# Quantising the last layer's weights during the expert layer, and loading them rounded

## Chip, cores and metric

One core of one Trainium2 chip runs the whole program in one launch. The metric is device time in microseconds (us), lower is better. The kernel before has a median of 3632.83 us over three runs (3630.29 to 3636.98).

## What is computed

x has 8 batches of 512 rows of 256 values; a context of 8 x 1024 x 192 is attended to. Four sublayers follow one another, each added to x after a layer norm: a cross attention of 16 heads, an expert layer (for each batch the two best of eight experts, chosen from the batch's first row, two 256 x 256 matrices each with GELU between), a second cross attention, and a quantised feed-forward layer, which is where the change begins:

```python
def quantize_w8_per(w, axis):
    amax = jnp.clip(jnp.max(jnp.abs(w), axis=axis, keepdims=True), 1e-08, None)
    scale = 127.0 / amax
    return jnp.clip(jnp.round(w * scale), -128.0, 127.0) / scale
...
W_in_sim = quantize_w8_per(W_in, axis=0)      # 256 x 1024
W_out_sim = quantize_w8_per(W_out, axis=1)    # 1024 x 256
x_sim = quantize_a16(x)                       # one scale for all of x
hidden = jax.nn.gelu(x_sim @ W_in_sim + b_in, approximate=False)
hidden_sim = quantize_a16(hidden)             # one scale for all of hidden
out = hidden_sim @ W_out_sim + b_out
```

The quantised weights depend on the inputs alone, so they can be made at any time before the layer.

## The kernel before, in words

`build` runs four functions one behind the other, each a block in which the five engines have their own instruction streams, tied by semaphores: `first_attention`, `experts` (L860), `second_attention` (L1112) and `quantised_layer` (L1721). All DMAs around the change are issued by SyncE (SP) on one queue.

**experts.** SyncE loads eight first rows for the routing (L926), x of batch 0 (L927), two small routing arrays (L928, L929) and x of the other seven batches, 512 KB each, which share one semaphore (L931). Then it waits for the routing, stores the chosen numbers as one row of 256 bytes (L935), waits for it and loads, batch by batch into two sets of buffers, the weights of two experts (L945 to L951). VectorE does the routing, normalises batch 0, and then in a loop normalises batch b+1 and updates batch b:

```python
with dve.Fori(0, B - 1) as b:
    normalise_batch(b + 1)
    update(b)
```

A normalisation is statistics (L72, L78, L81), a reciprocal root on GpSimd (L1086) and the scaling (L89). GpSimd then takes half of the second bias off x (L1097 to L1103). TensorE does for each batch: the hidden product (L987), the turning of the next batch's normalised rows (`turn_rows`, L973), the second product (L998). ScalarE applies GELU (L1025) and keeps the turned rows in SBUF (L1014). Batches go in pairs, in a loop of three with the last pair unrolled; TensorE's turned rows for batch b+1 need the normalisation that stands behind the update of batch b-1 on VectorE.

**second_attention.** In the last batch SyncE loads the turned first weight matrix, 1 MB, into the resident buffer `spare` (L1286), and it stores every batch's x as it is done (L1288).

**quantised_layer.** In its first block SyncE waits for the stores of x and loads x again (L1842 for batches 0 and 1, L1845 for the other six, under one semaphore), the two biases (L1847, L1848), and, once `spare` is free, the second matrix into it (L1851). VectorE first quantises the first matrix in `spare` (`quantise_weights`, L1731 to L1753: maximum per row, scale, eight multiplications L1746, clipping and rounding L1751 and L1753), then normalises the eight batches and takes their maxima (L72 to L1900). TensorE turns the rounded matrix in two halves of eight 128 x 128 transposes (L1861), each copied by ScalarE (L1880), and then the rows of x (L1872, L1883). After x's overall maximum (L1792 to L1808) the second block multiplies: VectorE rounds x (L1951, L1954) and splits off the low part (L1959), ScalarE makes the high part (L2008) and the GELU (L2014), TensorE the first projection (L1999). VectorE's order there is: batches 0 and 1 rounded and split, the second matrix quantised in `spare`, and then a loop that rounds batch b+2, takes the maxima of batch b's GELU (L1966) and splits batch b+2. The third block multiplies with the second matrix (L2186, L2188).

Of the kernel before, what the change touches and what calls it, by code (L numbers as in the profile page):

```python
# [5 lines left out]
F32 = mybir.dt.float32  # L6
# [7 lines left out]
P = 128  # L14
# [845 lines left out]
def experts(nc, x_sb, ident, mhalf, d, x_before):  # L860

    with ExitStack() as ctx:
# [33 lines left out]
        hT = sb("hT", [P, 2, FT, NQ])  # L896

# [21 lines left out]
        s_x = sem("x_updated")  # L919

# [3 lines left out]
        def _(sp):  # L924
# [12 lines left out]
            with sp.Fori(0, B // 2) as i:  # L937
                for u in range(2):

                    sp.wait_ge(s_x, QT * (2 * i + u))  # L940
                    for k in range(2):
# [10 lines left out]
                                     ).then_inc(s_w[u], 16)  # L952

        @block.tensor
        def _(pe):
# [11 lines left out]
            def turn_rows(b):  # L967
# [6 lines left out]
                mm.then_inc(s_tr, 1)  # L974

# [30 lines left out]
            with pe.Fori(0, B // 2 - 1) as i:  # L1006
                two_batches(i, False)
# [3 lines left out]
        def _(act):  # L1011
# [19 lines left out]
            with act.Fori(0, B // 2 - 1) as i:  # L1031
# [4 lines left out]
        def _(dve):  # L1036
# [37 lines left out]
            with dve.Fori(0, B - 1) as b:  # L1074
# [37 lines left out]
def second_attention(nc, x_sb, ident, ident_r, mhalf, d, ctx_parts, x_dram, spare, s_win, s_xs):  # L1112


    with ExitStack() as ctx:
# [112 lines left out]
        def _(sp):  # L1228
# [39 lines left out]
            def batch(b, left):  # L1268
# [452 lines left out]
def quantised_layer(nc, ident, ones, mhalf, d, x_dram, out, spare, s_win, s_xs):  # L1721
# [5 lines left out]
    with ExitStack() as ctx:  # L1727
        def sb(name, shape, dt=F32, to=ctx):
            return to.enter_context(nc.sbuf_tensor("f_" + name, shape, dt))

        def quantise_weights(dve, w, whole, top, s, inv, loaded, need, s_wq):  # L1731


            dve.wait_ge(loaded, need)
            nc.vector.tensor_reduce(top[:], w[:], AX.X, ALU.max, apply_absolute_value=True
                                    ).then_inc(s_wq, 1)
            dve.wait_ge(s_wq, 1)
            nc.vector.tensor_scalar(top[:], top[:], TINY, None, ALU.max).then_inc(s_wq, 1)
            dve.wait_ge(s_wq, 2)
            nc.vector.reciprocal(s[:], top[:]).then_inc(s_wq, 1)  # L1740
            dve.wait_ge(s_wq, 3)
            nc.vector.tensor_scalar(s[:], s[:], 127.0, None, ALU.mult).then_inc(s_wq, 1)
            dve.wait_ge(s_wq, 4)
            nc.vector.reciprocal(inv[:], s[:]).then_inc(s_wq, 1)
            for t in range(FFT):
                nc.vector.tensor_scalar(w[:, t, :], w[:, t, :], s[:, t:t + 1], -128.0,  # L1746
# [548 lines left out]
```

## Time and profile before

| | |
|---|---|
| median of 3 runs | 3632.83 us (3630.29 to 3636.98) |
| profiled execution, its own time | 3637.8 us |
| its span in the trace | 3635.9 us |
| TensorE busy, matmul | 3342.1 us (92% of the span) |
| VectorE | 2393.1 us (66%) |
| ScalarE | 1674.5 us (46%) |
| GpSimd | 1207.1 us (33%) |
| DMA | 379.08 MB, mean 104 GB/s |

PE is TensorE's matmuls, PEld its weight loads, DVE VectorE, ACT ScalarE, POOL GpSimd, and SPq the DMA instructions that SyncE issues. The span runs from the first to the last instruction of one profiled execution; the time of that execution is 1.9 us longer. The granted clock is 1.00 where TensorE runs at 2.4 GHz and 0.50 where it runs at 1.2 GHz; a number between is a stretch with both. The experts take the span from about 2109 to 2265 us, the second attention to 3384, the last layer the rest. A busy share is an average; which wait ends last is read from the timelines.

### The profile page before, as it was taken

The page shows a single profiled execution, that of the slowest core. Times are in us where ns is not written, and L with a number is a line of the kernel's source. Part 1 is how long each engine was busy: PE and PEld are TensorE (multiplying, and loading weights), DVE is VectorE, ACT ScalarE, POOL GpSimd, SP SyncE. Part 2 cuts the span into 40 slices and gives each one's busy share as a digit, 9 for nine tenths or more (in the row PEclk, how much of TensorE's full clock was granted, in tenths as well). Part 3 has the DMA queues.
Part 4 walks back from the last instruction along what each step waited for, and adds up shares of the span by engine and source line. Part 5 has one row for each costly group of instructions (what it writes and reads, how often), then busy time and mean ns, then how long its engine had stood idle before and what let it go on. Part 6 is the DMA issues. An engine that isn't in the chain of part 4 may idle for free. (4 is left out here: it accounts for less than half of the span.)

```text
span 3635.9 us, 49119 instructions
## 1 busy us (share of the span) xinstructions
PE 3342.1 (92%) x14300; PEld 1881.8 (52%) x14300; DVE 2393.1 (66%) x3634; ACT 1674.5 (46%) x1904; POOL 1207.1 (33%) x545
## 2 busy tenths in 40 slices
PE   6999999999999999999999868799999999999576
PEld 4445445455454464454464445455555555554366
DVE  4665665665656656656646524687788778777699
ACT  3442442443433433434434312366566566566376
POOL 2563663554645545636546613100000000000101
PEclk9999999999999999999999989799999999999698
DMA  7444544444534435535445232344344343343202
GB/s 183 122 119 117 121 121 103 121 109 126 121 101 123 120 101 133 122 99 125 108 118 128 68 110 79 75 105 106 72 102 104 79 103 96 89 101 82 65 18 75
DMA packets 265102, 379.08 MB, mean 104 GB/s; under 512 B 35944, under 2 KB 170672, under 8 KB 265008
## 3 DMA queue, kind: packets, MB, share of 16 engines
q1 hardware_dynamic: 265008, 378.06, 41.2%
q8 instruction: 31, 0.51, 0.1%
q14 instruction: 63, 0.52, 0.0%
HBM read 82.22 MB, written 27.26 MB: 30 GB/s over the span
## 5 line engine op out<-in xcount | busy, mean ns | idle before, releaser
L839 POOL TENSOR_TENSOR a_prob_sum<-a_prob_sum,a_prob 128x1024 f32<-128x1024 f32 x384 | 915.8, 2385 | 420.4 <-ACT a_prob L576 409.6
L576 ACT ACTIVATE a_prob<-a_t 128x1024 f32<-128x1024 f32 x512 | 518.8, 1025 | 752.9 <-PE a_t L430 739.5
L1590 DVE TENSOR_REDUCE a_mhalves<-a_m 128x1 f32<-128x512 f32 x1024 | 689.9, 688 | 188.2 <-PE a_m L1341 185.2
L718 DVE TENSOR_REDUCE a_mhalves<-a_m 128x1 f32<-128x512 f32 x1024 | 671.0, 688 | 165.0 <-PE a_m L397 161.8
L1502 ACT ACTIVATE a_prob<-a_t 128x1024 f32<-128x1024 f32 x512 | 498.3, 1023 | 145.5 <-PE a_t L1361 140.2
L397 PE MATMUL a_m<-a_kh_n,a_qz 128*128 128x512 f32 x1024 | 445.1, 457 | 64.1 <-DVE a_kl_n L707 29.3
L1341 PE MATMUL a_m<-a_vh,a_qz 128*128 128x512 f32 x1024 | 463.5, 464 | 36.6 <-DVE a_mhalves L1590 19.7
L437 PE MATMUL a_o<-a_prob,a_v_pair 128*64 128x512 f32 x2048 | 495.7, 605 | 0.0
L732 DVE RECIPROCAL a_recip<-a_x 128x512 f32<-128x512 f32 x64 | 214.8, 3357 | 349.0 <-PE a_x L446 349.0
L397 PEld LDWEIGHTS a_m<-a_kh_n,a_qz 128*128 128x128 f32 x1024 | 186.3, 192 | 367.9 <-DVE a_mhalves L718 223.5
L422 PE MATMUL a_t<-a_q_hl,a_k_hh 128*128 128x512 f32 x1024 | 360.3, 433 | 8.0 <-DVE a_x_res L787 8.0
L1341 PEld LDWEIGHTS a_m<-a_vh,a_qz 128*128 128x128 f32 x1024 | 189.9, 189 | 325.1 <-DVE a_mhalves L1590 246.6
L430 PE MATMUL a_t<-a_q_hm,a_k_lm 66*128 66x512 f32 x1024 | 326.8, 400 | 0.0
L1361 PE MATMUL a_t<-a_qs,a_vs 128*128 128x512 f32 x1024 | 323.2, 397 | 3.9 <-ACT a_prob L1502 3.6
L1703 POOL TENSOR_TENSOR a_rstd<-a_veps,mhalf 128x4 f32<-128x4 f32 x8 | 8.1, 1018 | 820.0 <-DVE a_veps L81 819.8
L1368 PE MATMUL a_o<-a_prob,a_v_all 128*18 128x512 f32 x2048 | 269.7, 598 | 0.4 <-ACT a_prob L1502 0.4
L422 PEld LDWEIGHTS a_t<-a_q_hl,a_k_hh 128*128 128x128 f32 x1024 | 191.0, 192 | 117.1 <-issue 74.6
L839 POOL TENSOR_TENSOR a_prob_sum<-a_prob 128x1024 f32<-128x1024 f32 x64 | 153.5, 2398 | 279.0 <-ACT a_prob L576 279.0
L437 PEld LDWEIGHTS a_o<-a_prob,a_v_pair 128*64 128x64 f32 x2048 | 124.2, 136 | 206.2 <-issue 166.0
L1361 PEld LDWEIGHTS a_t<-a_qs,a_vs 128*128 128x128 f32 x1024 | 191.7, 189 | 53.1 <-ACT a_prob L1502 14.4
L430 PEld LDWEIGHTS a_t<-a_q_hm,a_k_lm 66*128 66x128 f32 x1024 | 197.7, 193 | 35.6 <-ACT a_q_hm L594 0.5
L582 ACT CAST a_kh_n<-a_m 128x1024 fp32r<-128x1024 f32 x64 | 64.8, 1012 | 142.7 <-PE a_m L375 142.7
(242 smaller groups left out, 4081.2 us busy)
## 6 DMA issues: line engine op xcount, KB each, us to landing
a_k_hh<-a_kh_n SPq DMA_DIRECT2D x256, 256.0 KB, 4.5
a_k_lm<-a_kl_n SPq DMA_DIRECT2D x128, 256.0 KB, 4.2
a_v_pair<-a_v_all SPq DMA_DIRECT2D x64, 512.0 KB, 3.9
a_vs<-a_vh SPq DMA_DIRECT2D x256, 128.0 KB, 2.3
a_wk<-wk_parts SPq DMA_DIRECT2D x64, 256.0 KB, 3.5
a_q_hl<-a_qz SPq DMA_DIRECT2D x128, 128.0 KB, 3.3
a_q_hm<-a_qz SPq DMA_DIRECT2D x128, 128.0 KB, 3.7
a_q_hl<-a_ql_n SPq DMA_DIRECT2D x128, 128.0 KB, 4.2
```

Of the source, the lines that this page charges most:

```text
L397: pe.matmul(ps_m[:, n, :], qz[:, hd, qt * P:(qt + 1) * P], kh_n[:, n * 512:(n + 1) * 512], start=True, stop=True).then_inc(s_mx, 1)
L422: pe.matmul(ps_t[t % 2][:, hd, :], k_hh[:, u, hd, keys], q_hl[:, u, hd, :], start=True, stop=False)
L430: mm = pe.matmul(ps_t[t % 2][:, hd, :], k_lm[0:HD0 + 2, u, hd, keys], q_hm[0:HD0 + 2, u, hd, :], start=False, stop=True)
L437: mm = pe.matmul(ps_o[hd * HD0:(hd + 1) * HD0, :], v_pair[:, pr.set, t, hd * HD0:(hd + 1) * HD0], prob[:, t % RING, hd, :], start=(t == 0) ...
L576: nc.scalar.activation(prob[:, t % RING], ps_t[t % 2][:, :, :], ACT.Exp, scale=SCALE0).then_inc(s_exp, 1)
L718: nc.vector.tensor_reduce(mhalves[:, qt, hd, n:n + 1], ps_m[:, n, :], AX.X, ALU.max).then_inc(s_max, 1)
L839: nc.gpsimd.tensor_tensor(acc, prob[:, (t - 1) % RING] if t == 1 else acc, prob[:, t % RING], ALU.add).then_inc(s_acc, 1)
L1341: pe.matmul(ps_m[:, k, :], qz[:, u, h, qt * P:(qt + 1) * P], vh[:, u, k * 512:(k + 1) * 512], start=True, stop=True).then_inc(s_mx, 1)
L1361: mm = pe.matmul(ps_t[j][:, h, :], vs[:, u, 2 * j + h, keys], qs[:, u, 2 * j + h, :], start=True, stop=True)
L1368: mm = pe.matmul(ps_o[QD * h:QD * h + VW, :], v_all[:, t, GH * n + h, :], prob[:, t % RB, h, :], start=(t == 0), stop=(t == KT - 1))
L1502: nc.scalar.activation(prob[:, t % RB, 2 * j:2 * j + 2, :], ps_t[j][:, :, :], ACT.Exp, scale=SCALE1).then_inc(s_exp, 1)
L1590: nc.vector.tensor_reduce(mhalfs[:, u, qt, h, k:k + 1], ps_m[:, k, :], AX.X, ALU.max).then_inc(s_max, 1)
```

## The change

In `experts` SyncE now also loads both raw weight matrices (1 MB each), behind x and ahead of the chosen numbers. VectorE's loop is opened for the first two batches: it quantises the first matrix after the update of batch 0 and the second after that of batch 1. TensorE turns the first matrix behind the first pair of batches, in the PSUM tile that otherwise holds turned rows, with ScalarE copying. At the end SyncE stores both rounded matrices in device memory. In `second_attention` the load of the first matrix goes. In `quantised_layer` both quantisations, the turning and the load of the raw second matrix go; SyncE loads the two rounded matrices, 1 MB each, behind x and the biases. The scales' inverses stay in SBUF. `quantise_weights` itself is unchanged but for where it is defined.

```diff
@@ experts, SyncE
             for b in range(1, B):
                 sp.dma_start(x_sb[:, b * QT:(b + 1) * QT, :], x_view[:, b * QT:(b + 1) * QT, :]
                              ).then_inc(s_xrest, 16)
+            sp.dma_start(win_raw[:], d["winT"].rearrange("(t p) k -> p t k", p=P)).then_inc(s_wl[0], 16)
+            sp.dma_start(wout_raw[:], d["wout2"].rearrange("(t p) n -> p t n", p=P)).then_inc(s_wl[1], 16)
 
             sp.wait_ge(s_rt, 8)
             sp.dma_start(chosen_row[:], chosen[:]).then_inc(s_row, 16)
...
+            sp.wait_ge(s_wk, 2)
+            sp.dma_start(win_parts, win[:].bitcast(F32).rearrange("p c k -> p (c k)")).then_inc(s_win, 16)
+            sp.wait_ge(s_wq[1], 15)
+            sp.dma_start(wout_parts, wout[:].bitcast(F32).rearrange("p t n -> p (t n)")).then_inc(s_win, 16)
@@ experts, TensorE
+            def turn_weights():
+                pe.wait_ge(s_wq[0], 15)
+                pe.wait_ge(s_xnT, 3)
+                for r in range(2):
+                    pe.wait_ge(s_wk, r)
+                    for c in range(DCH):
+                        for t in range(4):
+                            mm = pe.transpose(ps_tr[:, c, t * P:(t + 1) * P],
+                                              win_raw[:, 4 * r + t, c * P:(c + 1) * P], ident[:])
+                    mm.then_inc(s_wt, 1)
+                pe.wait_ge(s_wk, 2)
...
-            with pe.Fori(0, B // 2 - 1) as i:
+            two_batches(0, False)
+            turn_weights()
+            with pe.Fori(1, B // 2 - 1) as i:
                 two_batches(i, False)
@@ experts, ScalarE
-            with act.Fori(0, B // 2 - 1) as i:
+            two_batches(0, False)
+            for r in range(2):
+                act.wait_ge(s_wt, r + 1)
+                nc.scalar.copy(win[:, :, r * 512:(r + 1) * 512], ps_tr[:]).then_inc(s_wk, 1)
+            with act.Fori(1, B // 2 - 1) as i:
                 two_batches(i, False)
@@ experts, VectorE
-            with dve.Fori(0, B - 1) as b:
+            normalise_batch(1)
+            update(0)
+            quantise_weights(nc, dve, win_raw, win_raw, win_max, win_s, win_inv, s_wl[0], 16, s_wq[0])
+            normalise_batch(2)
+            update(1)
+            quantise_weights(nc, dve, wout_raw, wout, wout_max, wout_s, wout_inv, s_wl[1], 16, s_wq[1])
+            with dve.Fori(2, B - 1) as b:
                 normalise_batch(b + 1)
                 update(b)
@@ second_attention, SyncE
-                else:
-
-                    sp.wait_ge(s_kq, 3 * NG * B)
-                    sp.dma_start(spare[:], d["winT"].rearrange("(t p) k -> p t k", p=P)).then_inc(s_win, 16)
@@ quantised_layer, first block
-                        sp.wait_ge(s_wt, 2)
-                        sp.dma_start(spare[:], d["wout2"].rearrange("(t p) n -> p t n", p=P)).then_inc(s_wout, 16)
-                        sp.wait_ge(s_wout, 48)
+                        sp.wait_ge(s_win, 32)
+                        sp.dma_start(win[:].bitcast(F32).rearrange("p c k -> p (c k)"), win_parts
+                                     ).then_inc(s_const, 16)
+                        sp.dma_start(wout[:].bitcast(F32).rearrange("p t n -> p (t n)"), wout_parts
+                                     ).then_inc(s_const, 16)
+                        sp.wait_ge(s_const, 64)
...
-                        for r in range(2):
-                            pe.wait_ge(s_wq, 15)
...
-                        quantise_weights(dve, spare, spare, win_max, win_s, win_inv, s_win, 16, s_wq)
@@ quantised_layer, second block
                     low(1, 1)
-                    quantise_weights(dve, spare, wout, wout_max, wout_s, wout_inv, s_mm, 1, s_wq2)
```

## Rows read from the trace of the kernel before

**Rows 1.** windows view, two stages: busy us per engine (x instructions), granted clock, DMA share, GB/s

```profile
2151.00:2183.00 32.00, 29.83 (x113) 19.50 (x112) 15.54 (x36) 8.69 (x11) 9.62 (x8) 1.00 0.27 82
...
3374.00:3400.00 26.00, 12.82 (x64) 8.64 (x56) 16.84 (x47) 4.70 (x6) 2.26 (x2) 0.74 0.55 180
```

**Rows 2.** timeline of one expert batch: start us, us, engine, line, operation, [idle before <- releaser]

```profile
2151.95 7.03 PE L987 MATMUL e_h<-e_xnT,e_w 128*128 x16
...
2152.25 0.43 DVE L1068 SCALAR_TENSOR_TENSOR x_sb<-e_y,x_sb 128x256 f32 x1 [1.30 <-PE e_y L998]
...
2155.96 4.18 DVE L89 TENSOR_SCALAR e_xn<-x_sb,e_mv,e_rstd 128x256 f32 x4 [1.13 <-POOL e_rstd L1086]
...
2160.20 1.09 PE L973 MATMUL e_tr<-ident,e_xn 128*128 128x128 f32 x8 [1.23 <-DVE e_xn L89]
...
2161.13 7.07 PE L998 MATMUL e_y<-e_w,e_hT 128*128 128x256 f32 x32
...
2168.35 0.42 DVE L1068 SCALAR_TENSOR_TENSOR x_sb<-e_y,x_sb 128x256 f32 x1 [1.30 <-PE e_y L998]
```

**Rows 3.** timeline, start of the experts: SyncE's DMA issues, VectorE and the first expert matmul

```profile
2110.44 7.89 SPq L931 DMA_DIRECT2D x_sb<-x_first  x7
...
2118.37 0.78 SPq L935 DMA_DIRECT2D e_chosen_row<-e_chosen  x1
...
2125.81 1.41 DVE L72 BATCH_NORM_STATS2 e_stats<-x_sb 128x6 f32 x4 [7.26 <-DMA x_sb<-x_first]
...
2126.16 0.41 SPq L945 DMA_DIRECT2D e_w<-in_w  x1
...
2133.96 10.20 PE L987 MATMUL e_h<-e_xnT,e_w 128*128 x16 [13.38 <-DMA e_b<-in_b]
```

**Rows 4.** windows view, one microsecond in which x is being loaded

```profile
2120.00:2121.00 1.00, 0.57 (x3) 0.17 (x1) 0.00 (x0) 0.39 (x1) 0.00 (x0) 0.50 1.11 350
```

**Rows 5.** timeline, start of the last layer: VectorE, TensorE, ScalarE and SyncE

```profile
3384.54 2.29 DVE L1735 TENSOR_REDUCE f_win_max<-spare 128x8 f32<-128x2048 f32 x1 [0.87 <-PEq L1115]
...
3392.21 1.40 DVE L72 BATCH_NORM_STATS2 f_stats<-f_hid 128x6 f32<-128x256 f32 x4
...
3392.35 1.97 PE L1861 MATMUL f_w<-ident,spare 128*128 128x128 f32 x8 [9.14 <-DVE spare L1753]
...
3397.49 1.01 ACT L1880 CAST f_win<-f_w 128x1024 fp32r<-128x1024 f32 x1 [2.12 <-PE f_w L1861]
...
3397.48 0.38 SPq L1851 DMA_DIRECT2D spare<-in_wout  x1
...
3401.47 1.41 DVE L72 BATCH_NORM_STATS2 f_stats<-f_hid 128x6 f32 x4 [2.78 <-DMA f_hid<-x_between]
```

**Rows 6.** timeline, the last layer's first projection: VectorE, ScalarE and TensorE

```profile
3445.62 2.28 DVE L1735 TENSOR_REDUCE f_wout_max<-spare 128x8 f32<-128x2048 f32 x1
...
3453.28 0.75 DVE L1951 TENSOR_SCALAR f_xnT<-f_xnT,f_amax_x  x1
...
3454.90 1.16 ACT L2008 ACTIVATE f_x_high<-f_xnT,f_minus_magic 128x1024 fp32r x1 [1.89 <-DVE f_xnT L1954]
...
3461.67 0.50 PE L1999 MATMUL f_h<-f_x_high,f_win 128*128 128x512 f32 x1 [0.96 <-ACT f_hid L2014]
...
3470.34 0.50 PE L1999 MATMUL f_h<-f_x_high,f_win 128*128 128x512 f32 x1 [0.96 <-ACT f_hid L2014]
```

**Rows 7.** windows view: stretches that show the granted clock fall and rise

```profile
2104.00:2109.00 5.00, 0.76 (x4) 0.33 (x2) 0.42 (x1) 0.00 (x0) 0.00 (x0) 1.00 0.31 105
...
2109.00:2110.00 1.00, 0.00 (x0) 0.00 (x0) 0.00 (x0) 0.00 (x0) 0.00 (x0) 0.72 0.03 8
...
2133.00:2140.00 7.00, 6.04 (x7) 2.52 (x8) 0.00 (x0) 1.97 (x2) 3.68 (x3) 0.50 0.66 188
...
2140.00:2144.00 4.00, 4.00 (x11) 1.71 (x10) 0.00 (x0) 1.37 (x2) 0.00 (x0) 0.98 0.01 4
...
3400.00:3403.00 3.00, 0.00 (x0) 0.00 (x0) 1.48 (x6) 0.60 (x1) 0.00 (x0) 1.00 1.11 343
```

More of the change, by code:

```diff
@@ L857, in _, with quantise_weights, experts @@
             batch(B - 1, True)
-def experts(nc, x_sb, ident, mhalf, d, x_before):
+def quantise_weights(nc, dve, w, whole, top, s, inv, loaded, need, s_wq):
+    dve.wait_ge(loaded, need)
+    nc.vector.tensor_reduce(top[:], w[:], AX.X, ALU.max, apply_absolute_value=True
+                            ).then_inc(s_wq, 1)
+    dve.wait_ge(s_wq, 1)
+    nc.vector.tensor_scalar(top[:], top[:], TINY, None, ALU.max).then_inc(s_wq, 1)
+    dve.wait_ge(s_wq, 2)
+    nc.vector.reciprocal(s[:], top[:]).then_inc(s_wq, 1)
+    dve.wait_ge(s_wq, 3)
+    nc.vector.tensor_scalar(s[:], s[:], 127.0, None, ALU.mult).then_inc(s_wq, 1)
+    dve.wait_ge(s_wq, 4)
+    nc.vector.reciprocal(inv[:], s[:]).then_inc(s_wq, 1)
+    for t in range(FFT):
+        nc.vector.tensor_scalar(w[:, t, :], w[:, t, :], s[:, t:t + 1], -128.0,
+                                ALU.mult, ALU.max).then_inc(s_wq, 1)
+    flat = w[:].rearrange("p t k -> p (t k)")
+    whole = whole[:].rearrange("p t k -> p (t k)")
+    dve.wait_ge(s_wq, 13)
+    nc.vector.tensor_scalar(flat, flat, 127.0, MAGIC, ALU.min, ALU.add).then_inc(s_wq, 1)
+    dve.wait_ge(s_wq, 14)
+    nc.vector.tensor_scalar(whole, flat, MAGIC, None, ALU.subtract).then_inc(s_wq, 1)
+def experts(nc, x_sb, ident, mhalf, d, x_before, win_parts, wout_parts, win_inv, wout_inv, s_win):
     with ExitStack() as ctx:
@@ L896, in experts @@
         hT = sb("hT", [P, 2, FT, NQ])
+        win_raw = sb("win_raw", [P, FFT, D])
+        wout_raw = sb("wout_raw", [P, FFT, D])
+        win = sb("win", [P, DCH, FF], F32R)
+        wout = sb("wout", [P, FFT, D], F32R)
+        win_max = sb("win_max", [P, FFT])
+        win_s = sb("win_s", [P, FFT])
+        wout_max = sb("wout_max", [P, FFT])
+        wout_s = sb("wout_s", [P, FFT])
         ps_tr = psum("tr", [P, DCH, NQ])
@@ L1109, in _, with second_attention @@
             two_batches(B // 2 - 1, True)
-def second_attention(nc, x_sb, ident, ident_r, mhalf, d, ctx_parts, x_dram, spare, s_win, s_xs):
+def second_attention(nc, x_sb, ident, ident_r, mhalf, d, ctx_parts, x_dram, spare, s_xs):
     with ExitStack() as ctx:
@@ L1729, in sb @@
             return to.enter_context(nc.sbuf_tensor("f_" + name, shape, dt))
[L1731 to L1746, printed above, removed]
-                                        ALU.mult, ALU.max).then_inc(s_wq, 1)
-            flat = w[:].rearrange("p t k -> p (t k)")
-            whole = whole[:].rearrange("p t k -> p (t k)")
-            dve.wait_ge(s_wq, 13)
-            nc.vector.tensor_scalar(flat, flat, 127.0, MAGIC, ALU.min, ALU.add).then_inc(s_wq, 1)
-            dve.wait_ge(s_wq, 14)
-            nc.vector.tensor_scalar(whole, flat, MAGIC, None, ALU.subtract).then_inc(s_wq, 1)
         def psum(name, shape, to=ctx):
@@ L1877, in _ @@
                     def _(act):
-                        for r in range(2):
-                            act.wait_ge(s_wt, r + 1)
-                            nc.scalar.copy(win[:, :, r * 512:(r + 1) * 512], ps_w[:]).then_inc(s_wk, 1)
                         with act.Fori(0, B) as b:
```

41 lines of the change are left out of this document (16 added, 25 removed).

## Prediction, made before the changed kernel was run

> **What bounds the kernel now.** I read the page first for the size of the whole, then a table of stages, then timelines of the two places that the change touches. The sum below is made against the profiled execution, 3637.8 us (span 3635.9); the median of the three runs shown is 3632.8, 5.0 us less, so what the sum adds is added to the median. 0.2%, about what a measurement of this kernel can tell from no change, is 7.3 us.
>
> The change takes work from the last layer and puts it into the experts. By busy share the experts look like a good home for vector work: in a stretch of two batches VectorE is busy 15.54 of 32 us, while where the last layer starts it is busy 16.84 of 26 us [rows 1]. The shares mislead in both places, and the timelines say why.
>
> In an expert batch one chain closes on itself [rows 2]. The last update of x for batch 0 starts at 2152.25; VectorE then normalises batch 2, its last scaling ending at 2160.14 (2155.96 + 4.18); TensorE turns those rows at 2160.20, after 1.23 us with nothing to do; the second expert product follows at 2161.13; and the next batch's last update starts at 2168.35. The period is 2168.35 - 2152.25 = 16.1 us. The hidden product (7.03 us from 2151.95) lies beside the normalisation and ends before it. So whatever VectorE does between an update and the next normalisation lengthens the chain in full, though VectorE stands idle elsewhere in it, for the second product.
>
> In the last layer the first quantisation runs from 3384.54 to 3392.21, 7.67 us, at the head of VectorE's work [rows 5]. But at 3401.47, before the statistics of batch 2, VectorE has waited 2.78 us for the loads of x. These six loads share one semaphore, so that time is set by the transfers and not by VectorE. The second quantisation runs from 3445.62 to 3453.28, 7.66 us, beside the first projection [rows 6]. There TensorE starts each batch 0.96 us after its own last product of the batch before, when the last GELU is done: 3461.67 and 3470.34 both show that wait, on ScalarE and not on VectorE.
>
> **The change part by part.**
>
> First, SyncE issues two loads of 1 MB (the raw weight matrices) in the experts between the loads of x and the load of the chosen experts' numbers. Now the last x loads are issued by 2118.33, the numbers at 2118.37; they arrive only just before 2126.16, when the first expert weights are issued, though they are 256 bytes [rows 3]. They stand behind the x bytes, which arrive for VectorE at 2125.81; the DMA engines were full then, 350 GB/s [rows 4]. Two more megabytes ahead of them are 2.10 MB / 350 GB/s = 6.0 us. TensorE's first expert product waited for the expert weights until 2133.96 [rows 3], so it starts at about 2140.0: **+6.0 us**. Bounds: 0, if the numbers slip past the bulk; 7.5, if the engines reach only 80% of that rate.
>
> Second, the quantisation of the first matrix stands on VectorE after batch 0's update and before the normalisation of batch 2. It is 15 instructions, the same as now, so 7.67 us [rows 5]. It is on the chain: TensorE turns batch 2's rows that much later, and all behind it (product, update, next normalisation) waits. **+7.7 us.** The second quantisation stands after batch 1's update and before the normalisation of batch 3: 7.66 us [rows 6], **+7.6 us** rounded down, as the hidden product of that batch, which now comes later, may take a little of it over. GpSimd has nothing to do in either stretch: its bias work for batch 1 stands behind the reciprocal root for batch 2, and so meets the scaling as now (4.18 us). Nothing of the 15.3 us is hidden. Lower bound 12, if 3 us somewhere find cover; above, 15.5.
>
> Third, TensorE turns the first matrix, 16 transposes in two halves, each followed by a copy on ScalarE, with TensorE waiting. In the last layer this takes from 3392.35 to 3398.50, 6.2 us [rows 5]. In the experts it follows batch 1's second product, while VectorE updates, quantises (7.7) and normalises (7.5): 15.8 us from that product's end. TensorE needs 6.2 + 7.0 for the next hidden product = 13.2. **0**, with 2.6 us to spare; if VectorE's work were not there, 6.2.
>
> Fourth, the clock. TensorE's hidden product of batch 1 ends at 2158.98 now, 2165.0 then, and the rows it turns next come at 2173.9: 8.9 us of nothing. In this trace 5 us with 0.76 us of work leave it at the full 2.4 GHz, and then it falls, 0.72 in the next microsecond [rows 7]; the same product at 1.2 GHz, before the clock rises at about 2140, takes 10.20 us [rows 3, 7] where it takes 7.03 at full clock [rows 2]. The rows' turning and the second product, which are on the chain, restart at the low level: I take **+3.0 us**, near that difference of 3.2. Bounds: 0 and 4.1 (3.2 and 0.9 for the eight transposes, 1.97 us [rows 5] against 1.09 [rows 2]).
>
> Fifth, two stores of 1 MB are issued at the experts' end, behind the last expert weights, which are issued when batch 5 is updated, so with two batches (2 x 16.1 us) still to run; 6.0 us of transfer: **0**, at most 6 if the next stage's first loads met them.
>
> Sixth, the last layer without the first quantisation, its 16 transposes and two copies. VectorE can take batches 0 and 1 earlier and then waits for the six loads until 3401.47 as before. The 7.67 us become waiting: 2.78 grows to some 9 or 10. **0.** The load of the second matrix, issued at 3397.48, is replaced by two of 1 MB issued some 1.5 us earlier, again behind x, and nothing needs them before the first projection. **0**; bounds 0 and +3, if the two took half of the rate while the last of x is in flight. The removed load in the second attention was hidden: 0.
>
> Seventh, the first projection without the second quantisation. ScalarE's high part for batch 2 waited 1.89 us for VectorE [rows 6] and no longer does, but it had made this up by 3461.67, as TensorE's wait there is the usual 0.96. **-0.1**, with bounds 0 and -1.9.
>
> **Sum:** 6.0 + 7.7 + 7.6 + 0 + 3.0 + 0 + 0 - 0.1 = +24.2 us: 3662.0 for an execution like the profiled one, **3657.0 from the median**.
>
> A rule that bears on the third and fourth term: the three blocks of eight transposes in the last layer were TensorE's only work since 3383, and after them the clock stands at 1.00 from 3400 to 3403 [rows 5, 7], so turning does raise it. The Trainium skill (TensorE: Matmul & The Clock Gate, Part 4: PE-mode transpose) says that the full clock doesn't engage for transposes, which don't count as a busy TensorE. By that rule TensorE would count as idle from batch 1's second product on, and the fourth rival below would be the forecast; the rows contradict it.
>
> **The rivals.**
> A (6%), faster: the experts have the cover. VectorE's idle half there [rows 1] takes both quantisations, the loads slip in, and the last layer gives back both: 3632.8 - 7.7 - 7.7 = 3617.4. Its place is the chain of rows 2: it holds only if TensorE's own work per batch is longer than normalisation plus quantisation, that is if the 1.23 us of waiting were more than 7.7 us of slack instead. And the return needs x to land by about 3394. Half of it would still be faster. The rows speak against both; I leave it 3% for the whole and 3% for a part that ends at no change.
> B (12%): the load of the numbers isn't held up by the matrices: 3657.0 - 6.0 = 3651.0. For it: the DMA engines are sixteen, and a small transfer uses few. Against: the numbers took from 2118.37 to about 2125 now.
> C (8%): x lands sooner or VectorE is the bound of the last layer's start after all. The gain is then what the quantisation took less its old wait, 7.7 - 2.8 = 4.9: 3652.1.
> D (12%): the clock falls a second time, between the matrix's turning (or the hidden product after it) and batch 3's rows, and the chain pays once more: 3657.0 + 3.0 = 3660.0.
>
> **How the numbers follow.** The forecast has 62%, the four rivals 38%. The likeliest case's own range is 3657.0 - 4 (clock at 0, some cover) to + 5 (dearer transfers, stores, clock), and some 0.1% for the spread of the runs. Taking in B, C and D the range is 3648 to 3665; outside are A and chances of a missed term. Slower by over 0.2% is above 3640.1: the forecast, B, C and D, 94%. No change: 3%. Faster: 3%.
>
> **What would show it.** Right: the first expert product at about +6 us against the row of before, the first weights issued at some 2132; gaps of about 8 us on TensorE before the rows of batches 2 and (about 2) 3, each with VectorE in the quantisation; the clock at 0.50 after the first; the experts longer by some 24 us; in the last layer a wait for x of 9 or 10 us before the statistics of batch 2, and the time from the last store of x to the end unchanged within 1 us. Wrong: quantisations that run while TensorE is at the second product, numbers that land at 2125 as now, or a last layer shorter by 5 us or more.

## The result, and the profile after

The changed kernel takes 3674.4 us, the median of 4 runs (3671.7 to 3677.6), against 3631.6 us before (3629.9 to 3637.0): a ratio of 1.0113, 95% interval 1.0098 to 1.0129, **1.1% slower**. The forecast was 3657.0 us, the range 3648 to 3665: right in its sign, and short by 17 us. The profiled execution after has a span of 3669.8 us against 3635.9. It was the fastest of the four after, and the one profiled before was slower than any of the four it is timed against, so the spans differ by 33.9 us where the medians differ by 42.9; the 9 us between the two are in no table below. All executions that the ratios of this document rest on are fast ones; one of run 7's four took 6628 us and is left out of its ratio, though not of its median.

Where the 33.9 us between the two profiled spans went, by the start of VectorE's last addition in each stage (first attention, experts, second attention, last layer), in us. For the first attention it is the first of its four closing additions, 10.3 us ahead of the last in every run, so those 10.3 us count with the experts throughout:

| | first attention ends | experts | second attention | last layer |
|---|---|---|---|---|
| before | 2094.5 | 168.9 | 1119.8 | 249.6 |
| after | 2094.9 | 190.1 | 1134.6 | 247.1 |
| after - before | +0.4 | **+21.2** | **+14.8** | -2.5 |
| forecast | 0 | +24.3 | 0 | -0.1 |

The experts came out 3.1 us under the forecast. The second attention, whose arithmetic the change does not touch, lost 14.8 us, and no term or rival had it: the one sentence of the forecast on that stage is that the load removed there was hidden, 0.

**The start of the experts.** SyncE's queue and TensorE's first rows, timelines of the kernel after (start, us, engine, line, operation, tiles, then idle time before and what ended it):

```profile
2118.32 1.33 SPq L970 DMA_DIRECT2D e_win_raw<-in_winT  x1
2119.69 3.30 SPq L971 DMA_DIRECT2D e_wout_raw<-in_wout  x1
2123.04 2.01 SPq L974 DMA_DIRECT2D e_chosen_row<-e_chosen  x1
2132.43 0.40 SPq L984 DMA_DIRECT2D e_w<-in_w  x1
```
```profile
2139.79 9.76 PE L1042 MATMUL e_h<-e_xnT,e_w 128*128 128x512 f32 x16 [18.85 <-DMA e_b<-in_b]
```

The numbers are issued at 2123.04 where it was 2118.37, the first weights at 2132.43 where it was 2126.16, and the first product starts 5.8 us later [rows 3]. Of 6.3 us of delay, 4.7 lie between the issues of x and that of the numbers, where the two new issues stand (1.33 and 3.30 us), and 1.6 behind it. An issue takes 0.40 us at 2132.43; whether the two are long because the queue is still full of x, and so an effect of the transfers, no run tells.

**The chain of the experts.** VectorE, then TensorE, in the same columns:

```profile
2157.54 0.42 DVE L1129 SCALAR_TENSOR_TENSOR x_sb<-e_y,x_sb 128x256 f32<-128x256 f32 x1 [1.30 <-PE e_y L1053]
2157.88 2.27 DVE L864 TENSOR_REDUCE e_win_max<-e_win_raw 128x8 f32<-128x2048 f32 x1
...
2164.39 1.23 DVE L882 TENSOR_SCALAR e_win_raw<-e_win_raw 128x2048 f32<-128x2048 f32 x1
2165.54 1.40 DVE L72 BATCH_NORM_STATS2 e_stats<-x_sb 128x6 f32<-128x256 f32 x4
...
2168.69 4.17 DVE L89 TENSOR_SCALAR e_xn<-x_sb,e_mv,e_rstd 128x256 f32<-128x256 f32 x4 [1.13 <-POOL e_rstd L1153]
...
2182.38 0.43 DVE L1129 SCALAR_TENSOR_TENSOR x_sb<-e_y,x_sb 128x256 f32<-128x256 f32 x1 [1.30 <-PE e_y L1053]
2182.72 2.28 DVE L864 TENSOR_REDUCE e_wout_max<-e_wout_raw 128x8 f32<-128x2048 f32 x1
...
2190.38 1.40 DVE L72 BATCH_NORM_STATS2 e_stats<-x_sb 128x6 f32 x4
```
```profile
2157.34 7.03 PE L1042 MATMUL e_h<-e_xnT,e_w 128*128 128x512 f32 x16
2172.92 1.97 PE L1016 MATMUL e_tr<-ident,e_xn 128*128 128x128 f32 x8 [8.55 <-DVE e_xn L89]
2174.68 7.66 PE L1053 MATMUL e_y<-e_w,e_hT 128*128 128x256 f32 x32
2182.17 1.04 PE L1026 MATMUL e_tr<-ident,e_win_raw 128*128 128x128 f32 x8
2184.31 1.09 PE L1026 MATMUL e_tr<-ident,e_win_raw 128*128 128x128 f32 x8 [1.10 <-ACT e_win L1091]
```

Each quantisation stands between an update and the next statistics (2157.88 to 2165.54, 2182.72 to 2190.38), 7.66 us each, and TensorE's wait ahead of batch 2's rows grows from 1.23 [rows 2] to 8.55. Now the period from update to update is 24.8 us (2157.54 to 2182.38) in place of 16.1 [rows 2].

TensorE's clock in five stretches of the kernel after. Behind the bounds and the length stand busy us (and instructions) of TensorE's matmuls, its weight loads, VectorE, ScalarE and GpSimd, then the granted clock as a share of 2.4 GHz, DMA share and GB/s:

```profile
2133.00:2145.00 12.00, 5.21 (x6) 2.18 (x7) 0.00 (x0) 1.97 (x2) 3.68 (x3) 0.50 0.70 219
2145.00:2150.00 5.00, 5.00 (x17) 2.52 (x16) 0.00 (x0) 1.79 (x3) 0.00 (x0) 0.99 0.02 6
2169.00:2175.00 6.00, 2.08 (x9) 2.08 (x10) 3.86 (x4) 0.08 (x1) 3.44 (x3) 0.50 0.00 0
2176.00:2186.00 10.00, 8.30 (x46) 7.03 (x44) 4.76 (x10) 1.57 (x2) 0.00 (x0) 1.00 0.14 39
2186.00:2192.00 6.00, 4.91 (x6) 2.19 (x7) 5.88 (x18) 1.14 (x2) 0.00 (x0) 0.51 0.52 157
```

It fell in the 8.55 us of waiting as expected, and again at 2186, behind the turning of the matrix. The first fall cost 1.97 - 1.09 us on the rows and 7.66 - 7.07 on the product. The second cost nothing, since the slow product lay beside VectorE's quantisation and normalisation.

**The last layer.** VectorE's first and third statistics in the kernel after:

```profile
3419.61 0.42 DVE L1725 TENSOR_TENSOR x_sb<-a_m,x_sb 128x256 f32<-128x256 f32 x1 [0.44 <-PE a_m L1523]
...
3427.35 1.41 DVE L72 BATCH_NORM_STATS2 f_stats<-f_hid 128x6 f32<-128x256 f32 x4 [7.31 <-DMA f_hid<-x_between]
...
3438.89 1.41 DVE L72 BATCH_NORM_STATS2 f_stats<-f_hid 128x6 f32 x4 [5.05 <-DMA f_hid<-x_between]
```

The 7.67 us of quantisation have turned into waits for x, 7.31 and 5.05 us where there was one of 2.78 [rows 5], and batch 2's statistics start 19.3 us behind the last addition where it was 18.2 (3401.47 - 3383.25). The 2.5 us that this stage still won are luck. VectorE's first result for the last batch but one starts 240.0 us behind the second attention's last addition in both kernels; over the 7 us of the last products the clock is 0.51 before (3625 to 3632) and 1.00 after (3659 to 3666).

**The second attention.** VectorE at the turn of its loop over the batches (five turns), first before, then after:

```profile
2733.17 0.75 DVE L1662 TENSOR_TENSOR x_sb<-a_m,x_sb 128x256 f32 x2
2735.17 3.27 DVE L1590 TENSOR_REDUCE a_mhalves<-a_m 128x1 f32<-128x512 f32 x5 [1.26 <-PE a_m L1341]
```
```profile
2759.79 0.75 DVE L1725 TENSOR_TENSOR x_sb<-a_m,x_sb 128x256 f32 x2
2763.49 1.29 DVE L1653 TENSOR_REDUCE a_mhalves<-a_m 128x1 f32<-128x512 f32 x2 [2.95 <-issue]
```

A wait of 2.95 us that no semaphore ends ("issue") stands where 1.26 us for TensorE stood. TensorE then waits for VectorE, and its clock halves for some 7 us. TensorE's wait after, then the stretch of 7 us before and after:

```profile
2764.24 0.79 PE L1404 MATMUL a_m<-a_vh,a_qz 128*128 128x512 f32 x1 [1.78 <-DVE a_mhalves L1653]
```
```profile
2735.00:2742.00 7.00, 6.21 (x27) 3.06 (x26) 4.99 (x8) 5.14 (x5) 0.00 (x0) 1.00 0.66 165
```
```profile
2763.00:2770.00 7.00, 5.76 (x19) 3.55 (x19) 4.63 (x7) 4.95 (x5) 0.00 (x0) 0.52 0.65 172
```

A looped batch takes 136.4 us in place of 133.7; five such turns give 13.0 of the 14.8 us, and the other 1.8 lie outside them. The table of transfers of one such batch has a line in the kernel after that it has not in the kernel before:

```profile
q14 instruction: 5, 0.04, 0.1%
```

five fetches of instructions, of 8192 bytes each by their records. Over the whole execution the page counts 88 of them on this queue (0.72 MB) against 63 (0.52 MB): 25 more, five for each of five turns. Between two such fetches VectorE has 131 and 125 records in the trace. That suggests pieces of 128 instructions of 64 bytes, an estimate from these two counts and the 8192 bytes. By a count of VectorE's program the loop body has 354 instructions and begins at instruction 672 before and at 738 after; the traces don't hold this count, but show 363 VectorE records in a turn of either kernel. The 66 instructions more in front of it are not the quantisations alone: in the trace these are 30 records (their waits are part of them), and the first two batches' normalisations and updates, which the change writes out ahead of the experts' loop, are 39 more. That gave the theory that most of the runs below test: **a body that lies in three pieces stays in the engine's store, one that reaches into a fourth is fetched anew in every turn**.

### The profile page after: what moved, and what is told of

The parts are those of the page before. It is cut to its first block and busy times, and to the rows that moved or that the text cites. A ratio compares the mean times of both kernels' runs of the same rounds, so it can differ in the third digit from the quotient of the medians.

```text
span 3669.8 us, 49055 instructions
## 1 busy us (share of the span) xinstructions
PE 3349.9 (91%) x14300; PEld 1889.4 (51%) x14300; DVE 2395.1 (65%) x3634; ACT 1674.5 (46%) x1902; POOL 1208.0 (33%) x545
```

## The experiments

Each kernel was timed against the kernel before on the same chip. The median of the latter was 3633.8 us for runs 1, 2, 3 and 6, 3635.6 for runs 4, 5, 7 and 8, and 3634.9 for runs 9 to 12. The writes of one element go to a tile that nothing reads and take 0.06 us each. The stages are those of the table above, each from one profiled execution; in the seven kernels here whose second attention shows no fetches it takes 1120.1 to 1122.5 us, so 2 us in it mean nothing:

| | median | ratio (95%) | first ends | experts | second | last |
|---|---|---|---|---|---|---|
| after, 62 writes | 3656.2 | 1.0064 (1.0047 to 1.0081) | 2092.4 | 190.1 | 1121.7 | 246.0 |
| before, 66 writes | 3649.2 | 1.0039 (1.0024 to 1.0053) | 2094.3 | 169.1 | 1133.8 | 247.3 |
| before, 20 writes | 3648.5 | 1.0039 (1.0025 to 1.0054) | 2091.4 | 167.8 | 1135.6 | 248.1 |
| before, 128 writes | 3635.1 | 1.0007 (0.9997 to 1.0017) | 2091.7 | 167.8 | 1121.9 | 247.1 |
| before, 45 + 83 writes | 3595.1 | 0.9890 (0.9873 to 0.9906) | 2051.9 | 167.4 | 1122.5 | 249.4 |
| after, loads behind | 3658.6 | 1.0071 (1.0055 to 1.0088) | 2090.0 | 184.3 | 1128.9 | 247.6 |
| after, quantised early | 3660.1 | 1.0065 (1.0044 to 1.0085) | 2095.3 | 179.0 | 1134.6 | 246.6 |
| after, all three | 3651.7 | 1.0050 (1.0033 to 1.0066) | 2093.6 | 184.0 | 1120.1 | 246.1 |
| before, own semaphores | 3631.4 | 0.9989 (0.9980 to 0.9998) | 2092.6 | 168.0 | 1121.8 | 243.2 |
| after, own semaphores | 3670.7 | 1.0092 (1.0076 to 1.0107) | 2095.8 | 193.7 | 1134.6 | 242.3 |
| change repaired | 3596.2 | 0.9892 (0.9877 to 0.9907) | 2055.0 | 176.7 | 1120.1 | 241.7 |
| before, best | 3588.3 | 0.9867 (0.9851 to 0.9882) | 2055.7 | 167.5 | 1121.8 | 242.1 |

**1. The kernel after, its loop body put back** (VectorE, experts, ahead of the wait for the other batches' x; the same edit with another count in the three runs after it):

```diff
             normalise_batch(0)
+            for n in range(62):
+                nc.vector.memset(filler[:, n:n + 1], 0.0)
             dve.wait_ge(s_xrest, 16 * (B - 1))
```

> The kernel after, with 62 one-element writes to a tile that nothing reads put on VectorE in the experts, ahead of its wait for the rest of x. They move VectorE's later instructions back by 62, so that the loop body of the second attention (354 instructions) begins at the same place modulo 128 as in the kernel before (instruction 800 of the stream against 672; in the kernel after it begins at 738). Theory A (the 14.8 us that the second attention lost come from the loop body's place in the instruction stream, which has five pieces of it fetched anew in every batch): looped batches back from 136.4 to 133.7 us, no fetches of instructions inside the loop, TensorE's clock at 1.0 in it, 3674.4 - 14.8 = 3659.6 us. Theory B (the loss comes from the new buffers' places in SBUF or from the matrices' stores and loads): batches stay at 136.4 us, 3674.4 us.

The second attention took 1121.7 us in place of 1134.6, and the extra wait at the turn is gone:

```profile
2752.45 0.75 DVE L1728 TENSOR_TENSOR x_sb<-a_m,x_sb 128x256 f32 x2
2754.46 3.26 DVE L1656 TENSOR_REDUCE a_mhalves<-a_m 128x1 f32<-128x512 f32 x5 [1.26 <-PE a_m L1407]
```

The page counts 63 fetches again, as before the change. All buffers, stores and loads of the change are still there, so theory B falls. 13.0 us of the 14.8 came back; the rest is within what the stage differs by between kernels without fetches.

**2. The kernel before with 66 writes.** It has nothing of the change but the count of instructions.

> The kernel before, nothing of the change in it, with 66 such one-element writes at the same place, so that the second attention's loop body on VectorE begins at instruction 738, as in the kernel after. Theory A (place in the instruction stream): fetches inside the loop, looped batches of 136.4 us in place of 133.7, TensorE's clock at 0.5 for 6.8 us in each, 3631.6 + 14.8 = 3646.4 us. Theory B (buffers or transfers of the change): batches of 133.7 us, 3631.6 us; the writes themselves lie in an idle time of VectorE.

It is slower by 0.39%, some 14 us, nearly all in the second attention (1133.8). Its turn shows the wait:

```profile
2740.97 1.29 DVE L1593 TENSOR_REDUCE a_mhalves<-a_m 128x1 f32<-128x512 f32 x2 [3.02 <-issue]
```

**3. The kernel before with 128 writes.**

> The kernel before with 128 such writes: the loop body begins at instruction 800, the same place modulo 128 as 672. Theory A, if what counts is the place within pieces of 8 KB: 3631.6 us, at most 1 us more where the writes outlast the idle time, and batches of 133.7 us. Theory A', if what counts is that anything was moved, or how many instructions lie ahead: as with 66 writes, +14.8 us, 3646.4 us. Theory B (buffers or transfers): 3631.6 us as well; the run with 66 writes tells B from A.

No loss: what counts is the place within a piece, not how much stands in front.

**4. The kernel before with 20 writes.**

> The kernel before with 20 one-element writes in the experts. By the counts of VectorE's records between two fetches the loop body of the second attention begins 17 instructions behind a border and ends 13 ahead of one in the kernel before. Theory A (borders of 128 instructions, three pieces stay, four don't): moved by 20 the body reaches into a fourth piece, five fetches a batch, batches of 136 us, time 3631.6 + 14.8 = 3646.4 us as with 66. Theory A' (the loss grows with how far the body reaches into the fourth piece): some 1.5 to 5 us. Theory B (a threshold elsewhere between 20 and 66): 3631.6 us.

The full loss already (1135.6 us, 88 fetches), not a part of it: being over the border by 7 instructions costs what being over by 53 costs (20 and 66 less the 13 of the expectation's count). By the theory, then, either part of the change's 66 instructions would have cost the whole loss alone.

```profile
2738.40 1.29 DVE L1593 TENSOR_REDUCE a_mhalves<-a_m 128x1 f32<-128x512 f32 x2 [3.01 <-issue]
```

**5. The first attention's loop body, put in three pieces** (VectorE, ahead of its first wait; 83 more writes in the experts keep the second body's place):

```diff
+            for n in range(45):
+                nc.vector.memset(filler0[:, n:n + 1], 0.0)
             dve.wait_ge(s_first, 32)
```

> The kernel before with 45 one-element writes on VectorE ahead of its first wait and 83 in the experts. The second attention's loop body keeps its place modulo 128 (45 + 83 = 128); that of the first attention (309 instructions, which in the kernel before has five pieces of the stream fetched anew in every batch, and VectorE waiting 2.63 us for nothing but instructions at its turn) moves back by 45 and then lies in three pieces of 128 in place of four. Theory A (a body in three pieces stays in the engine's store, one in four is fetched anew each time): the fetches in the first attention's loop go, and 6 or 7 turns lose some 2.6 us of VectorE's wait each, of which TensorE sees most: 3631.6 - 15 = 3616 us, between 3613 and 3624 us. Theory B (the fetches there belong to another engine, or the second attention's case was about something else): fetches stay, 3631.6 us.

1.1% **faster than before**, 40 us where 15 were expected; the first attention ends 42.6 us sooner. VectorE at a turn before, GpSimd beside it, then VectorE and GpSimd with the edit:

```profile
578.63 1.40 DVE L72 BATCH_NORM_STATS2 a_stats<-a_ctx_raw 128x6 f32<-128x256 f32 x4 [2.63 <-issue]
...
582.42 7.63 DVE L89 TENSOR_SCALAR a_xn<-a_ctx_raw,a_mv,a_rstd 128x256 f32<-128x256 f32 x4 [1.13 <-POOL a_rstd L820]
```
```profile
582.34 2.38 POOL L839 TENSOR_TENSOR a_prob_sum<-a_prob 128x1024 f32<-128x1024 f32 x1
```
```profile
568.57 1.41 DVE L72 BATCH_NORM_STATS2 a_stats<-a_ctx_raw 128x6 f32<-128x256 f32 x4
...
571.73 3.47 DVE L89 TENSOR_SCALAR a_xn<-a_ctx_raw,a_mv,a_rstd 128x256 f32<-128x256 f32 x4 [1.13 <-POOL a_rstd L823]
```
```profile
572.67 2.39 POOL L842 TENSOR_TENSOR a_prob_sum<-a_prob 128x1024 f32<-128x1024 f32 x1 [0.97 <-ACT a_prob L577]
```

The page counts 34 fetches in place of 63. Each of the six turns is 7.1 us shorter, not 2.6. The wait for instructions is 2.63 + 0.51 us of it. The other 4.2 are the four scalings, 7.63 us before and 3.47 now: three of the four took 2.5 us and one 0.40, now one takes 2.5 and three 0.41. Before, they began at 582.42, as GpSimd began its sums over probabilities (582.34, 2.38 us each), and kept step with them; without the wait three of the four have started when GpSimd begins at 572.67, and only the fourth takes 2.5 us. The Trainium skill (SBUF — State Buffer, SBUF: two separate sides) says that VectorE and GpSimd share a port pair, which some forms of VectorE's instructions need, and that the one that starts first holds it for its whole instruction while the other fully blocks. The durations in step with GpSimd's 2.4 us agree; that these scalings are of such a form is not shown, and no run but this one changes how the two engines lie to each other, so the collision as the cause of the 4.2 us is argued from the times.

**6. The two loads behind the first pair's weights** (SyncE; two_batches is the loop's body):

```diff
-            sp.dma_start(win_raw[:], ...).then_inc(s_wl[0], 16)
-            sp.dma_start(wout_raw[:], ...).then_inc(s_wl[1], 16)
...
+            two_batches(0)
+            sp.dma_start(win_raw[:], ...).then_inc(s_wl[0], 16)
+            sp.dma_start(wout_raw[:], ...).then_inc(s_wl[1], 16)
+            with sp.Fori(1, B // 2) as i:
+                two_batches(i)
```

> The kernel after with the loads of the two raw matrices (1 MB each) issued behind the weights of the first pair of every batch of the first two, in place of ahead of the chosen experts' numbers. Theory A (the two loads and their issue delay the first expert weights by 5.5 us net, the first term of the forecast): first expert product back from 2139.8 to about 2134.3 us, time 3674.4 - 5.5 = 3668.9 us. Theory B (the delay comes from the numbers' own transfer, or comes back later as bandwidth taken from the third and fourth batch's weights): 3674.4 us. The second attention keeps its 136.4 us a batch in both.

The experts are 5.8 us shorter, as theory A has it. The time fell by more, some 15 us, and the profile puts the rest elsewhere: 4.9 us, most of it in the loads at the very start of the kernel, which differ by up to 5 us between executions, and 5.8 us in the second attention. There VectorE has the same wait at every turn and five fetches in each, and the page counts 90, but the clock behaves differently from turn to turn. The second turn's wait with the 10 us around it, then the start of the third turn:

```profile
2614.22 3.96 DVE L1658 TENSOR_REDUCE a_mhalves<-a_m 128x1 f32<-128x512 f32 x6 [2.98 <-issue]
```
```profile
2611.00:2621.00 10.00, 7.13 (x31) 4.26 (x32) 6.04 (x10) 5.27 (x6) 0.15 (x1) 1.00 0.67 166
```
```profile
2750.00:2754.00 4.00, 4.00 (x13) 2.31 (x16) 2.72 (x5) 2.56 (x3) 0.00 (x0) 0.57 0.73 197
```

The five turns take 135.8, 134.3, 135.5, 135.8 and 136.6 us. In the second the clock doesn't fall, in the last it is down for some 7 us as in the kernel after (136.4), and in the other three for less than 4. Beside 133.7 us without fetches, the wait alone thus costs 0.6 us and the fallen clock up to 2.3 more: most of the loss is the clock's. The turns together are 3.7 us shorter than those of the kernel after, and the other 2.1 lie outside them. Why the same wait brings the clock down in one turn and not in another isn't settled.

**7. Both quantisations ahead of the first update** (VectorE):

```diff
             normalise_batch(1)
+            quantise_weights(..., win_raw, ...)
+            quantise_weights(..., wout_raw, ...)
             update(0)
-            quantise_weights(..., win_raw, ...)
             normalise_batch(2)
             update(1)
-            quantise_weights(..., wout_raw, ...)
```

> The kernel after with both quantisations of raw matrices moved ahead of the first expert update, into the 16.9 us in which VectorE waits there for the first expert products. Theory A (each quantisation between two updates stands whole on the chain of VectorE's updates, the second term of the forecast): the last update of the first two batches 7.7 and 8.7 us sooner, 16.2 us in all; the turning of the first matrix, which now stands between the rows of two batches, may come to the surface with 0 to 6 us. Time 3674.4 - 16.2 = 3658.2 us, up to 3664 us. Theory B (the chain has slack: TensorE or the weights' transfers end last): under 3 us of gain, above 3671 us. The second attention keeps its 136.4 us a batch in both.

The experts took 179.0 us, 11.1 less than after. The quantisations are off the chain, and the matrix's turning is on it: TensorE's second product ends at 2173.5 and the next hidden product starts only at 2178.30.

```profile
2131.17 2.28 DVE L864 TENSOR_REDUCE e_win_max<-e_win_raw 128x8 f32<-128x2048 f32 x1
...
2148.10 1.23 DVE L882 TENSOR_SCALAR e_wout<-e_wout_raw 128x2048 fp32r<-128x2048 f32 x1
2152.73 0.42 DVE L1129 SCALAR_TENSOR_TENSOR x_sb<-e_y,x_sb 128x256 f32<-128x256 f32 x1 [3.41 <-PE e_y L1053]
```
```profile
2178.30 8.83 PE L1042 MATMUL e_h<-e_xnT,e_w 128*128 x16 [1.59 <-ACT e_win L1091]
```

So 10.0 us more than before are left: the loads' 5.5 and 4.8 for the turning (2173.5 to 2178.3).

**8. The three edits together** (1, 6 and 7).

> The kernel after with three edits together: the raw matrices' loads behind the first pair's weights, both quantisations ahead of the first update, and 62 one-element writes on VectorE that put the second attention's loop body at instruction 800, the place modulo 128 that it has before. Theory A (the three costs are separate and are all that the change costs): 5.5 + 16.2 + 14.8 = 36.5 us less than 3674.4, plus 0 to 6 us where the turning of the matrix comes to the surface: 3637.9 to 3643.9 us, within 0.4% of the kernel before. Theory B (what is saved in the experts is taken back by another wait there, such as the matrices' load that arrives later than the quantisation wants it): above 3648 us.

Theory B. The second attention is whole again (1120.1), but the experts take 184.0 us: the loads, moved behind the weights, land too late for the early quantisations,

```profile
2143.70 2.29 DVE L864 TENSOR_REDUCE e_win_max<-e_win_raw 128x8 f32<-128x2048 f32 x1 [14.43 <-DMA e_win_raw<-in_winT]
```

which end at 2159.1 (2157.89 + 1.23), while TensorE had its hidden product done at 2156.3, so that batch 2's rows come at 2167.73 after 11.48 us of waiting for VectorE. Each of the two edits alone takes 5.8 and 11.1 us off the experts, together 6.1.

**9 and 10. One semaphore for each batch's x in the last layer**, on the kernel before and on the kernel after (three lines and the loop that they replace):

```diff
-            s_xl = [sem("x_loaded0"), sem("x_loaded1"), sem("x_loaded")]
+            s_xl = [sem(f"x_loaded{b}") for b in range(B)]
...
-                        dve.wait_ge(s_xl[2], 16 * (B - 2))
-                        with dve.Fori(0, B // 2 - 1) as i:
+                        for b in range(2, B):
+                            dve.wait_ge(s_xl[b], 16)
```

> The kernel before with one semaphore for each batch's x in the last layer in place of one for batches 2 to 7 (VectorE's loop over them written out). Theory A (the last layer's start is set by the x loads that count as landed only together): the wait of 2.78 us ahead of batch 2's statistics goes, 3631.6 - 2.8 = 3628.8 us. Theory B (the start is set by something behind it, such as the maximum over all batches that waits for TensorE's turning): 3631.6 us, within 0.5 us.

> The kernel after with the same edit. Theory A (the quantisation that the change took out of the last layer's start gained nothing because the x loads under one semaphore set the time): now the 5.05 us of wait ahead of batch 2's statistics go, 3674.4 - 5.0 = 3669.4 us, more than the same edit gives on the kernel before (2.8). Theory B (the x loads themselves, one by one, are as late): 3674.4 us.

On the kernel before the medians differ by 3.5 us where 2.8 were expected; the interval of the ratio allows 0.7 to 7.3. Batch 2's statistics follow with no wait, in the kernel before and then in the kernel after with this edit:

```profile
3397.73 1.40 DVE L72 BATCH_NORM_STATS2 f_stats<-f_hid 128x6 f32<-128x256 f32 x4
```
```profile
3431.78 1.40 DVE L72 BATCH_NORM_STATS2 f_stats<-f_hid 128x6 f32<-128x256 f32 x4 [7.21 <-DMA f_hid<-x_between]
...
3438.19 1.40 DVE L72 BATCH_NORM_STATS2 f_stats<-f_hid 128x6 f32<-128x256 f32 x4
```

On the kernel after, the last layer is 4.8 us shorter (247.1 to 242.3), the 5.0 expected. The time can't confirm it: the median moved by 3.7 us, the ratio from 1.0113 to 1.0092, some 7.6, and the profiled execution hardly at all, as its experts took 3.6 us more. With both kernels so edited the last layer differs by 0.9 us (243.2 and 242.3): even then the removed quantisation of 7.7 us is worth about 1, as the first x load sets the start in its place (7.21 us of waiting).

**11. The change repaired**: after, with 5's writes (45 and 17), 7 and 10.

> The kernel after with both quantisations ahead of the first update, a semaphore for each batch's x in the last layer, and 45 + 17 one-element writes on VectorE that put the loop bodies of both attentions where each lies in three pieces of the instruction stream. Theory A (the costs are those found, one by one): the kernel before with its two bodies placed so measured 3595.1; to it come 10 us in the experts (what the change with early quantisations cost there) and -5 to -7.5 in the last layer: 3598 to 3600 us, so that the change still doesn't pay against the kernel before with the same places. Theory B (the stages work on each other, the costs don't add up): off that by more than 5 us.

3596.2 us, 2 us under the range of theory A. Each saving holds beside the others here. Against the kernel before with the same two places (3595.1) it still gains nothing: 9.3 us lost in the experts (176.7 against 167.4) for 7.7 won in the last layer, and of these the semaphores alone give most (run 9: 243.2 against 241.7 here).

**12. The same aim elsewhere**: the kernel before with 5 and 9, and this call in the second attention, its function moved out of the last layer:

```diff
                 elif n > 0:
                     keep_o(G - 1)
                     divide(G - 1, n - 1)
+                    quantise_weights(nc, dve, spare, spare, *win_q, s_win, 16, s_wq)
```

> None of the change's stores, but its aim in another place: the kernel before with the first matrix quantised by VectorE in the last head group of the second attention, where it waits some 18 us for TensorE, with a semaphore for each batch's x in the last layer, and with 45 + 83 one-element writes for the two loop bodies' places. Theory A (the quantisation hides there, and the last layer's start is then limited by x alone): 3595.1 - 2.8 - 1.9 = 3590.4 us. Theory B (it delays the second attention's last copies, or x's arrival sets the start whatever VectorE does): 3592 to 3600 us.

3588.3 us, **the fastest of all, 1.33% under the kernel before**. The quantisation runs from 3318.57, and VectorE still waits 10.25 us for TensorE behind it, where the kernel before has 17.91. First the kernel before, then this one:

```profile
3376.43 0.72 DVE L1605 STREAM_TRANSPOSE a_o_rows<-a_o 128x512 f32<-128x512 f32 x1 [17.91 <-PE a_o L1368]
```
```profile
3318.57 2.28 DVE L1122 TENSOR_REDUCE win_max<-spare 128x8 f32<-128x2048 f32 x1
...
3336.56 0.72 DVE L1636 STREAM_TRANSPOSE a_o_rows<-a_o 128x512 f32<-128x512 f32 x1 [10.25 <-PE a_o L1399]
```

The second attention is not longer (1121.8). Most of the gain over before is run 5's; the semaphores and the moved quantisation add some 7 us by the medians. The moved quantisation has little part in this: the last layer takes 242.1 us with it and 243.2 with the semaphores alone (run 9). Hiding this work costs nothing here, and gains about 1 us.

## Why the prediction was right, and where it was wrong

- **First term, the loads ahead of the numbers, +6.0.** Measured 5.8 from row to row, less 0.4 of shift brought along; run 6 gives back 5.8. The size is right. The make-up is open: the term was worked out as bytes over a rate, while in the trace 4.7 us of the delay stand at the two issues (1.33 and 3.30) on SyncE's queue, which may or may not be long for the transfers' sake. Rival B, numbers not held up, falls.
- **Second term, +7.7 and +7.6.** 7.66 each, whole on the chain, as run 7 confirms by taking them off. Rival A, that the experts have cover, falls in the place where the change put them. The cover lies a step earlier: ahead of the first update VectorE waits 22.06 us for TensorE in the kernel after.
- **Third term, the turning hidden at 0, 6.2 if uncovered.** Hidden; uncovered in run 7 at 4.8.
- **Fourth term, the clock, +3.0 out of 0 to 4.1.** It fell as said, and was over-sized: 0.9 on the rows and 0.6 on the product, where 3.2 for a whole product had been taken, less 0.4 on the first product (9.76 against 10.20 [rows 3]). All of the experts without loads and quantisations is 21.2 - 5.5 - 15.3 = 0.4. Rival D happened and cost nothing; and it was after the turning that the clock fell, not through it: 1.00 from 2176 to 2186, with most of the turning in it. That turning raises the clock rests on the one rise that the prediction names; in the kernel before, from 3403 to 3420, turned rows were again TensorE's only work (7.06 us of 17), and the clock stood at 0.50.
- **Fifth term, 0.** The stores at the experts' end show nowhere: run 1, which has them, has its second attention and its last layer as long as the kernels without them.
- **Sixth term, 0.** Right: the quantisation became waiting, 12.4 us in two places where 9 or 10 in one were expected, and batch 2's statistics came 1.1 us later, inside the bound of 3. Rival C falls.
- **Seventh term, -0.1.** Right within what the profile can tell: the two last layers run level until their very end, and the 2.5 us there are the clock's, by luck.
- **The step that failed** is one not taken. The part by part went through the work that the change moves on each engine and queue, and of the stage between them it said only that the removed load was hidden, 0. What a longer instruction stream does to a loop behind it was no term and no rival, so the second attention stood at 0 without an argument. It lost 14.8 us, 12 to 14 of them by the place of its loop body: 1134.6 to 1121.7 when the body is put back (run 1), and 1121.9 to 1133.8 and 1135.6 when the kernel before has it moved (runs 3, 2 and 4). With that body put back the kernel after took 3656.2 us, 22.4 more than the kernel before beside it, where 24.2 had been forecast. The 1.8 us between them are inside the interval of that ratio.

## What to carry to other kernels

Adding instructions to one stage can slow a loop in another. Before timing a change, count each engine's instructions up to every long loop and look at the page's lines for instruction fetches; and when a stage that was not touched moves, read its loop's turn for a wait that nothing releases. Measure such a change with the loops' places held fixed, or its own cost is mixed with an accident of place (here some 13 of 34 us). And put vector work where the engine waits for something that can't be helped, not where its busy share is low: the same 7.7 us cost 7.7 between an update and a normalisation, and nothing in the last head group.

## What the runs showed of the hardware that was not expected

In both attentions, a looped body on VectorE that by the count lies in three pieces of 128 instructions is not fetched again in its loop. One that reaches into a fourth is fetched in every turn, five pieces of 8192 bytes, with some 3 us of waiting at the branch back (2.95, 3.02, 3.01 and 2.63 us in four kernels). Bodies of 354 and 309 instructions behave alike, and 20 instructions of shift are enough to go from one to the other. That the store holds four pieces, one of them fetched ahead, would explain the five and the border, but is worked out from the counts and not tested by itself. No other engine was tested. In the kernel before neither queue of instruction fetches shows one from 2451 to 3136 us, which holds the last five of the six batches of the second attention's loop, though TensorE has 889 records in each of them. What the wait sets off can be dearer than the wait: in the second attention 0.6 us a turn for the wait and up to 2.3 for a clock at half, and in the first, where a collision with GpSimd is the likely cause, scalings of 3.5 us that took 7.6.
